# Scores of the last 128 keys: high keys meet high and low queries in one product, and VectorE adds the halves

## What is computed

```python
x = x + attn(layernorm(x)); x = x + xattn(layernorm(x)); x = x + ffn(layernorm(x))
# in attn, per sequence b and head h (q already scaled by 128 ** -0.5):
sim = einsum('bhid,bhjd->bhij', q, k)
sim = tanh(sim / 50.0) * 50.0
sim = where(causal_mask, -max, sim)      # key j counts for queries i >= j
out = einsum('bhij,bhjd->bhid', softmax(sim), v)
```

## Time and profile before

| | |
|---|---|
| median of 3 runs (lowest to highest) | 1578.02 us (1577.18 to 1578.02) |
| the profiled execution: time, span | 1577.97 us, 1576.2 us |
| granted TensorE clock, mean over the span | 1.000 |
| PE busy | 1555.3 us, 99% |
| DVE busy | 1040.1 us, 66% |
| ACT busy | 583.2 us, 37% |
| POOL busy | 454.0 us, 29% |

### The profile page before, as it was taken

How to read it: one execution, slowest core, us unless ns; L and a number is a source line. 1 busy time by engine, 2 the same in 40 slices (tenths; PEclk the granted TensorE clock), 3 DMA queues, 4 the chain that set the end, 5 groups by cost and what they waited for, 6 DMA issues and landing times.

```text
span 1576.2 us, 23814 instructions
## 1 busy us (share of the span) xinstructions
PE 1555.3 (99%) x7776; PEld 1332.2 (85%) x7777; DVE 1040.1 (66%) x2230; ACT 583.2 (37%) x997; POOL 454.0 (29%) x390
## 2 busy tenths in 40 slices
PE   7999999999999999999999999999999999999998
PEld 5888888888888888888888888888888889999997
DVE  4798877788887788886787778755663662222222
ACT  4444443434444334444344344333212213333232
POOL 4445332134222233222233221113200013332431
PEclk9999999999999999999999999999999999999999
DMA  8786764677876686985686877366440256677643
GB/s 294 280 314 222 231 222 137 238 291 261 305 286 221 243 313 233 309 311 196 246 308 250 307 280 307 118 218 198 131 151 9 110 209 199 192 238 241 193 80 74
DMA packets 106804, 353.28 MB, mean 224 GB/s; under 512 B 11280, under 2 KB 31760, under 8 KB 101200
## 3 DMA queue, kind: packets, MB, share of 16 engines
q1 hardware_dynamic: 93488, 314.20, 55.4%
q0 software_dynamic: 13216, 37.79, 10.2%
HBM read 227.97 MB, written 123.98 MB: 223 GB/s over the span
## 4 chain that ended last, share of the span: by engine, by line
PE 92%; DVE 3%; DMA 2%; issue 1%; POOL 1%; ACT 1%; SPq 0%; DVEq 0%; ACTq 0%; POOLq 0%
PE bank L370 30%; PE bank L372 29%; PE bank L371 29%; PE bank L1984 1%; PE bank L2104 1%; DMA out<-x_early,ids_e 1%; DMA wqk<-wqk_parts 0%; DMA rows<-x_rows,ids_e 0%; DMA resid<-x 0%; POOL store L691 0%; DVE resid L1498 0%; DMA resid<-out 0%; DVE place_hot L1661 0%; DVE tile_vals L1671 0%; PE bank L2061 0%
## 5 line engine op out<-in xcount | busy, mean ns | idle before, releaser
L733 POOL TENSOR_TENSOR probs<-probs,causal 128x256 f32<-128x256 f32 x126 | 90.2, 737 | 408.9 <-ACT probs L913 408.9
L372 PE MATMUL bank<-store,wqk 128*128 128x512 f32 x512 | 202.1, 395 | 0.0
L370 PE MATMUL bank<-store,wqk 128*128 128x512 f32 x512 | 201.8, 394 | 0.2 <-DMA wqk<-wqk_parts 0.2
L371 PE MATMUL bank<-store,wqk 128*128 128x512 f32 x512 | 201.8, 394 | 0.0
L1304 DVE SCALAR_TENSOR_TENSOR resid<-bank,factor,resid 128x512 f32<-128x512 f32 x256 | 189.2, 741 | 1.2 <-PE bank L372 1.1
L691 POOL TENSOR_TENSOR pre_split<-pre_raw,pre_split 128x1528 fp32r<-128x1528 f32 x34 | 120.3, 3539 | 142.8 <-ACT pre_split L875 142.8
L911 ACT ACTIVATE probs<-bank 128x512 f32<-128x512 f32 x189 | 85.9, 529 | 130.8 <-PE bank L372 130.8
L372 PEld LDWEIGHTS bank<-store,wqk 128*128 128x128 f32 x512 | 96.0, 188 | 22.8
L371 PEld LDWEIGHTS bank<-store,wqk 128*128 128x128 f32 x512 | 96.1, 188 | 20.8
L370 PEld LDWEIGHTS bank<-store,wqk 128*128 128x128 f32 x512 | 96.0, 188 | 20.2 <-DMA wqk<-wqk_parts 0.4
L1335 DVE TRANSPOSE_TENSOR_REDUCE bank<-probs 128x16 f32<-128x512 f32 (+3 forms) x256 | 108.4, 492 | 0.0
(11 more groups left out here) (352 smaller groups left out, 3927.0 us busy)
## 6 DMA issues: line engine op xcount, KB each, us to landing
pre_parts<-pre_split SPq DMA_DIRECT2D x34, 1528.0 KB, 6.6
wqk<-wqk_parts SPq DMA_DIRECT2D x96, 512.0 KB, 4.9
pre_raw<-pre SPq DMA_DIRECT2D x34, 764.0 KB, 7.8
store<-wv_parts SPq DMA_DIRECT2D x12, 2048.0 KB, 9.1
wo<-wo_parts SPq DMA_DIRECT2D x48, 512.0 KB, 8.3
expert_w<-pre_parts SPq DMA_DIRECT2D x8, 2816.0 KB, 11.4
wqk_parts<-wqk SPq DMA_DIRECT2D x16, 1024.0 KB, 5.1
expert_w<-pre_parts SPq DMA_DIRECT2D x8, 1536.0 KB, 8.8
```

The lines of the kernel that those rows point to most:

```text
L370: nc.tensor.matmul(out_ap, a_hi, b_hi, start=first, stop=False)
L371: nc.tensor.matmul(out_ap, a_hi, b_lo, start=False, stop=False)
L372: return nc.tensor.matmul(out_ap, a_lo, b_hi, start=False, stop=last)
L733: nc.gpsimd.tensor_tensor(diagonal, diagonal, causal[:, :, :], ALU.mult).then_inc(S["masked"], 1)
```

## The change

Chunk 3 of the keys is no longer a triple. The high and low queries now lie in one tensor, `q_parts`, and one product of 256 columns takes the high keys of chunk 3 to the last 128 high queries and the last 128 low ones, side by side, into columns 256 to 511 of bank 4. A second product of 128 columns adds the low keys by the high queries to the first half. These two come first, then chunks 0, 1 and 2. VectorE gets a new instruction at the start of each turn, `sum_scores`, ahead of `turn_xn` and `q_lo`: it waits for `s_ready` and adds the two halves into the place of chunk 3 in bank 3. ScalarE waits for that (`s_summed`) ahead of its second tanh, the one of bank 3. `LAST_PARTS` are the same three ranges that were written out in `softmax_part`.

```diff
-        q_hi, q_lo, k_hi, k_lo = (sb(n, [P, SEQ], F32R) for n in ("q_hi", "q_lo", "k_hi", "k_lo"))
+        q_parts = sb("q_parts", [P, 2, SEQ], F32R)
+        q_hi, q_lo = q_parts[:, 0, :], q_parts[:, 1, :]
+        k_hi, k_lo = (sb(n, [P, SEQ], F32R) for n in ("k_hi", "k_lo"))
@@ softmax_part(u); the two added lines of the wait stand in softmax_last() too
-                for i, (lo, n) in enumerate(((0, SEQ), (SEQ, SEQ), (2 * SEQ, 2 * P))):
+                for i, (lo, n) in enumerate(LAST_PARTS):
+                    if i == 1:
+                        act.wait_ge(S["s_summed"], u + 1)
                     nc.scalar.activation(probs[:, lo:lo + n], bank[2 + i][:, 0:n], ACT.Tanh, scale=SCALE / SOFTCAP).then_inc(S["tanh_done"], 1)
@@ VectorE
+            def sum_scores(u):
+                dve.wait_ge(S["s_ready"], u + 1)
+                nc.vector.tensor_reduce(bank[3][:, SEQ - P:], bank[4][:, 2 * P:].rearrange("p (a n) -> p n a", a=2), mybir.AxisListType.X, ALU.add).then_inc(S["s_summed"], 1)
@@ VectorE, the loop over u
+                if u:
+                    sum_scores(u - 1)
                 if xnT_slot(u) is not None:
                     turn_xn(xnT_slot(u), 2, u)
                 lo_part(q_lo[:, :], bank[0][:, :], q_hi[:, :], "qk_hi_done", "q_lo_done", 2 * u + 1)
@@ behind the loop
+            sum_scores(U - 1)
             p_last()
@@ scores(u)
-                for j in (0, 1, 3, 2):
-                    to = bank[2 + POFF[j] // SEQ][:, POFF[j] % SEQ:POFF[j] % SEQ + SEQ - P * j]
-                    last = triple(to, k_hi[:, j * P:j * P + P], k_lo[:, j * P:j * P + P], q_hi[:, j * P:], q_lo[:, j * P:], True, True)
+                keys = lambda k, j: k[:, j * P:j * P + P]
+                nc.tensor.matmul(bank[4][:, 2 * P:], keys(k_hi, 3), q_parts[:, :, 3 * P:], start=True, stop=False)
+                nc.tensor.matmul(bank[4][:, 2 * P:3 * P], keys(k_lo, 3), q_hi[:, 3 * P:], start=False, stop=True)
+                for j in (0, 1, 2):
+                    last = triple(bank[2 + j][:, 0:SEQ - P * j], keys(k_hi, j), keys(k_lo, j), q_hi[:, j * P:], q_lo[:, j * P:], True, True)
                 last.then_inc(S["s_ready"], 1)
```

More of the change, by code:

```diff
@@ L263, in build @@
         pre_loaded pre_hi pre_lo pre_stored
-        q_ready k_ready vt_ready s_ready pv_ready y_ready
+        q_ready k_ready vt_ready s_ready s_summed pv_ready y_ready
         qk_hi_done v_hi_done o_hi_done tanh_done exp_done
```

## The result

The changed kernel takes 1619.65 us (median of 4 runs, 1618.82 to 1620.52) against 1577.6 of the kernel before in the same comparison (4 runs, 1577.07 to 1578.02): the ratio is 1.0263, with a 95% interval from 1.0251 to 1.0275. It is 42 us slower, inside the range, where 57.5 had been forecast. The profiled execution took 1620.52, with a span of 1618.8 at a granted clock of 0.998.

The account below looks back on a forecast made before the run. The prediction took TensorE's matmul stream to bound the kernel. Turn losses of 57.8 us, net of TensorE's saving, less 0.3 for units 0 and 1, added 57.5 to 1577.97: 1636 us, range 1614 to 1665.

Parts of the forecast that it names:

- What bounds, and the cover: TensorE's matmul stream bounds the kernel; in a plain turn VectorE may be 0.83 us later before output 3 stops.
- S = L - 0.83: At output 3, VectorE lateness L stops TensorE for S, whatever exceeds 0.83 us; plain turns S = 0.38.
- TensorE's part: Score products to next Q product: 0.54 instead of 0.70 us, saving 0.16 in each of 64 units, 10.2 in all.
- VectorE's part: The new reduce `sum_scores` takes 0.61 us: 0.42 plus 256 x 0.74 ns for summed elements lying apart.
- The rival with free jumps: Reading elements that lie apart in PSUM costs nothing extra, `sum_scores` takes 0.42 us: 1626 us; chance 0.25.
- The upper bound: `sum_scores` takes 1.11 us, like the transposition of 512 elements, called the loop's dearest single instruction: 1665 us.
- Where it lands: `sum_scores` waits behind `y_factors`; second tanh comes 1.40 us later, 1.56 against TensorE; a plain turn gets +0.22.
- The feedback: TensorE's stop at output 3 leaves VectorE free earlier against the next scores, by at most 0.35 us.
- The sum over the loop: Losses of all kinds of turn come to 57.8 us, less 0.3 for units 0 and 1: plus 57.5.
- the three turns of F = 1.80: Three more turns, with VectorE free 1.80 us behind the start of the Q projection: 1.2 us lost together.
- What would show it: Trace marks: reduce of about 0.6 us behind the reciprocal, second tanh near 2.2, TensorE idle some 0.4 in plain turns.
- On time: Rival: the sum comes before the cover ends, VectorE's lateness stays hidden, the saving is whole: 1568 us; chance 0.05.

Follow-up runs that it names:

- the early sum: Changed kernel with `sum_scores` of each unit moved into its own turn, ahead of the previous unit's softmax factors: 1579.95 us, ratio 1.0004.
- the sum alone: Changed kernel with the old three products for chunk 3, into bank 4, keeping the sum and its wait: 1620.0 us, ratio 1.0263.
- the sum twice: Changed kernel with the sum made twice, the second waiting for the first one's end: 1647.58 us, ratio 1.0433.

## Why the prediction was right, and where it was off

- **What bounds, and the cover.** Right. The loss vanishes when the sum leaves that place, and is there in full without any saving on TensorE. In turn 58 `q_lo` is 1.00 late (4.61 - 3.61). By the rule S = L - 0.83 TensorE stops for 0.17; the turn is 0.18 longer than with the early sum (15.00 - 14.82).
- **TensorE's part.** "a saving of 0.16 for each of 64 units" was too much: 0.10, from 1.92 (892.41 to 894.33, first product of the scores to next Q product, before) to 1.82 (932.34 to 934.16, after). The 0.06 went to the product of 512 columns behind a short one (0.29 for 0.23); output 3 showed that already in the kernel before (906.58 to 906.87, behind the products of 128 columns of `values`). As the forecast said of such a 0.06, it hardly mattered: with VectorE setting the pace the saving is worth nothing (the run of the sum alone).
- **VectorE's part: the term that was mis-sized.** "I take 0.42 + 256 x 0.74 ns = 0.61, since the pattern is that of the row of 381 ns." The two groups after:
```profile
L1355 DVE TENSOR_REDUCE bank<-bank 32x16 f32<-32x256 f32 x64 | 26.9, 420 | 2.2
L1334 DVE TENSOR_REDUCE bank<-bank 128x128 f32<-128x256 f32 x64 | 26.3, 411 | 2.4 <-PE bank L374 2.2
```
  The sum takes 0.411, no more than neighbours in PSUM do, and also 0.411 in the run of the sum alone, where both addends are the same element. The price of jumps was carried from a row in SBUF to a read from PSUM, though a row of PSUM stood beside it. Whether it is the memory or the pattern that differs (here pairs, there sums of 8), no run separates. The Trainium skill, page "PSUM — Partial Sum Buffer", section "Specifications (TRN2)", gives PSUM lines of 8 bytes and says that patterns without neighbours slow matmuls. The prediction stretched that rule to this read; the run does not agree with the stretch, and it decides. The rival with free jumps, 1626, was the better sum. The upper bound had a misreading too: the transposition with its 1.11 is not the dearest instruction of the loop, `p_lo` (L1312) takes 1.49; the measured 0.411 is near neither.
- **Where it lands: a cover that was overlooked.** "Exp and `q_hi` follow without a pause" read 3.61 as the end of ScalarE's chain. But `q_hi` also needs the last Q product. Timeline of TensorE, turn 58, before:
```profile
896.88 0.39 PE L372 MATMUL bank<-store,wqk 128*128 128x512 f32 x1
```
  It ends at 897.27, and `q_hi` started at 897.31: both ended there together. After, the product is long done, and `q_hi` starts 0.10 before exp's record ends (938.16 against 938.26). From second tanh to `q_lo` it is 2.69 after and 2.84 before, so 0.15 less of the lateness reaches `q_lo`.
- **The feedback.** Right as a rule, smaller in size. With a lateness of 1.56 - 0.20 for the price - 0.15 for `q_hi` - 0.06 for the saving = 1.15 and the forecast's own relation, S = L - 0.83 and L = 1.15 - S, L is 0.99; measured 1.00. The plain turn is then 0.16 - 0.10 = +0.06; turn 58 shows +0.09, against +0.22 forecast.
- **The sum over the loop.** Price and `q_hi` together are 0.35 in each late turn; in 41 of them that is 14.4. Taken from 57.5 that leaves 43, before the smaller plain turns: the loop and turn 63 show 42.3. By parts: layer norm, with the three turns of F = 1.80, 19.6 + 1.2 + 7.7 = 28.5 forecast, 20.95 measured, so 7.6 less, about 0.35 in each of 21 turns; turns 2 to 6 13.2 and 10.83; transposed tiles 7.6 and 5.31; the last three turns 3.7 and 3.30 (0.62, 1.35 and 1.33). The 18 plain turns of the forecast are the 15 of the table, 15 x 0.22 = 3.3 forecast and 1.00 measured, and those behind the gates, 0.7 + 1.3 = 2.0 and 1.29 (turns 15, 31 and 47, 0.43 each). That the 0.35 does not come off evenly in the other parts was not followed up. Turn 5 alone is not settled: +3.87 after, +2.65 with the sum alone, +4.31 with the sum twice.
- **What would show it.** In kind every mark came: the records of 256 and 128 columns, the reduce right behind the reciprocal, the late second tanh, the stops at the outputs released by `resid`, up to 2.7 at the routing. In size they were smaller: 1.92 for the second tanh instead of 2.2, and 0.2 for the stop of a plain turn instead of 0.4.
- **On time, the rival of a gain.** Its point, that the sum would have to come before the cover ends, is what the early sum does; its price, 1568, was not reached by any version, because the saving was 0.10, the early sum costs 4.05 in the routing turns, and weights came late.

## What to carry to other kernels

An instruction that a fast chain now has to wait for costs first what stands ahead of it in its queue, and, once that has used up the cover, its own length as well: here 64 sums of 0.41 us cost 42 us behind the chain of factors, some 70% of it still with a sum of 0.16, and 26 more in the loop with a second sum. Ahead of the chain, where their engine is idle, they stopped no output outside the routing turns but one in turn 13, which stops without any sum too. Ask for each kind of turn which engine sets the pace: a shorter matmul stream pays only where TensorE does, and there the next thing that was just in time (here a weight load) takes part of the gain. And where two things end together, the chain that was read is not the only one; the other gives cover that shows only when the first gets late.

## What the runs showed of the hardware

- VectorE's reduce of pairs 128 columns (512 bytes) apart in PSUM took 0.411 us, the same as with both addends at one place, while in SBUF summed elements that lie apart cost 0.381 against 0.286.
- A reduce of 8 elements per partition took 0.158, so some 0.25 of the 0.411 are its elements: 1.02 ns for each of 248.
- A ScalarE instruction whose input was long ready started 0.10 before the end of the record of the one before it (`q_hi` after exp).
- The product of 512 columns behind one of 128 needed 0.05 to 0.06 more to the next start (0.29) than behind another of 512.
